# Wide attention of layer 1: value rows as the stationary side, 512 turned probabilities as the moving side

## The reference, cut to what matters

```python
q = (query @ Wq + bq).reshape(b, sq, N_HEAD, KEY_DIM)
k = (key @ Wk + bk).reshape(b, key.shape[1], N_HEAD, KEY_DIM)
v = (value @ Wv + bv).reshape(b, value.shape[1], N_HEAD, VALUE_DIM)
scores = jnp.einsum('bqhd,bkhd->bhqk', q, k) / TEMP
attn = jax.nn.softmax(scores, axis=-1)
out = jnp.einsum('bhqk,bkhd->bqhd', attn, v).reshape(b, sq, N_HEAD * VALUE_DIM)
out = out @ Wo + bo + residual
mu = jnp.mean(out, axis=-1, keepdims=True)
var = jnp.var(out, axis=-1, keepdims=True)
return (out - mu) * jax.lax.rsqrt(var + EPS) * ln_gamma + ln_beta
```

## Time and profile before

| | |
|---|---|
| median of 3 runs | 1587.16 us (1586.48 to 1588.48) |
| the profiled execution, its own time | 1588.14 us |
| its span | 1586.3 us |
| TensorE matmul busy | 1302.4 us (82%) |
| VectorE, ScalarE, GpSimd busy | 954.0 us, 716.6 us, 533.3 us |
| mean granted TensorE clock | 0.894 of full speed |
| layer 1 attention in the span | 286 us to 601.5 us |

### The profile page before, as it was taken

How to read it: one execution, slowest core, us unless ns; L and a number is a source line. 1 busy time by engine, 2 the same in 40 slices (tenths; PEclk the granted TensorE clock), 3 DMA queues, 4 the chain that set the end, 5 groups by cost and what they waited for, 6 DMA issues and landing times. The chain is left out here.

```text
span 1586.3 us, 26220 instructions
## 1 busy us (share of the span) xinstructions
PE 1302.4 (82%) x9426; PEld 800.9 (50%) x9426; DVE 954.0 (60%) x2171; ACT 716.6 (45%) x1922; POOL 533.3 (34%) x625
## 2 busy tenths in 40 slices
PE   3799629679989877786996798989987978996998
PEld 2444317457767765464442455555644434442443
DVE  6466631455656654267564688888674865655664
ACT  3254413266656523343543465656655333454222
POOL 2320250534333251334000365657543320000444
PEclk8599859799999987896998799999987996998999
DMA  2444020330000002322000000000000001000000
GB/s 63 125 135 127 30 78 26 70 81 11 1 1 2 1 24 66 88 60 50 16 3 1 1 1 1 1 1 1 1 1 1 1 11 21 10 2 1 7 7 14
DMA packets 66997, 45.37 MB, mean 29 GB/s; under 512 B 17564, under 2 KB 60262, under 8 KB 66870
## 3 DMA queue, kind: packets, MB, share of 16 engines
q1 hardware_dynamic: 61013, 34.48, 8.4%
q0 software_dynamic: 4096, 8.40, 2.1%
q10 hardware_dynamic: 1760, 0.82, 0.3%
HBM read 24.91 MB, written 13.89 MB: 24 GB/s over the span
## 5 line engine op out<-in xcount | busy, mean ns | idle before, releaser
L3413 ACT ACTIVATE L2a_pr<-psum,L2a_negmax 128x512 f32<-128x512 f32 (+3 forms) x256 | 132.2, 531 | 94.0 <-DVE L2a_negmax L3539 40.1
L556 ACT ACTIVATE L1x_praw<-psum,L1x_negmax 128x154 f32<-128x154 f32 x256 | 96.2, 390 | 78.1 <-DVE L1x_negmax L649 78.1
L318 POOL TENSOR_TENSOR L1x_pm<-L1x_praw,L1x_total 128x1024 f32<-128x1024 f32 x32 | 60.8, 1899 | 161.2 <-DVE L1x_total L655 138.2
L3278 PE MATMUL psum<-ident,L2a_pr 128*128 128x128 f32 x640 | 87.7, 282 | 20.2 <-DVE L2a_pT L3552 12.9
L3278 PEld LDWEIGHTS psum<-ident,L2a_pr 128*128 128x128 f32 x640 | 73.1, 145 | 25.9 <-issue 23.4
L1980 POOL TENSOR_TENSOR L3f_scaled<-L3f_sg,L3f_wide 128x512 f32<-128x512 f32 (+1 forms) x44 | 55.8, 1272 | 66.8 <-ACT L3f_sg L2059 37.9
L1613 DVE TENSOR_REDUCE L3x_negmax<-psum 128x6 f32<-128x924 f32 (+1 forms) x48 | 47.7, 1011 | 46.7 <-PE psum L1151 37.4
L1613 DVE TENSOR_REDUCE L0x_negmax<-psum 128x6 f32<-128x924 f32 (+1 forms) x48 | 47.7, 1009 | 44.9 <-PE psum L1151 40.6
L419 PE MATMUL psum<-L1x_vw,L1x_pT 128*128 128x128 f32 x512 | 69.8, 293 | 3.0 <-DVE L1x_y L672 3.0
L3166 POOL TENSOR_TENSOR L2a_pr<-L2a_pr,L2a_total 128x768 f32<-128x768 f32 x32 | 48.7, 1522 | 69.9 <-DVE L2a_total L3568 69.7
L3163 POOL TENSOR_TENSOR L2a_pr<-L2a_pr,L2a_total 128x1024 f32<-128x1024 f32 x29 | 56.6, 1951 | 46.1 <-DVE L2a_total L3568 46.0
(11 more groups left out here) (741 smaller groups left out, 3406.3 us busy)
## 6 DMA issues: line engine op xcount, KB each, us to landing
expert_arena<-in_L_ffn_w SPq DMA_DIRECT2D x16, 256.0 KB, 4.5
group_in<-zero SPq DMA_DIRECT2D x2, 1472.0 KB, 9.3
L1f_xs<-group_in SPq DMA_DIRECT2D x10, 256.0 KB, 4.0
group_out<-L1f_ys SPq DMA_DIRECT2D x10, 256.0 KB, 2.3
L1f_gu<-in_L_ffn_gate_up_w SPq DMA_DIRECT2D x8, 256.0 KB, 3.4
slots_in<-zero SPq DMA_DIRECT2D x1, 1280.0 KB, 9.3
L0f_xs<-slots_in SPq DMA_DIRECT2D x5, 256.0 KB, 3.9
resid<-in_x SPq DMA_DIRECT2D x4, 256.0 KB, 5.9
```

The costliest lines, as they stand in the source:

```text
L318: nc.gpsimd.tensor_tensor(pm[:, n % 2].rearrange("p j t k -> p (j t) k"), praw[:, n % 3, :, :, 0:MAIN].rearrange("p j t k -> p (j t) k"), ...
L556: nc.scalar.activation(praw[:, n % 3, j, t, :], psum[:, 2 * u + j, x * CTX:(x + 1) * CTX], ACT.Exp, bias=negmax[:, n % 2, u, j, x:x + 1], ...
L3278: last = nc.tensor.transpose(psum[:, TURN + n // 4, n % 4 * P:(n % 4 + 1) * P], pr[:, m % RING, n * P:(n + 1) * P], core.ident[:])
L3413: ins = nc.scalar.activation(pr[:, i % RING, SEQ * j + lo:SEQ * j + hi], psum[:, bank + j, lo:hi], ACT.Exp, bias=negmax[:, i % RING, e:e + ...
```

## The change

The roles of the two operands of the value products are exchanged. The table `vw` of a head (128 context rows by 128 columns) becomes the stationary side, and the turned probabilities `pT` (128 context rows by 512 query rows) move past it in one go. One product takes the place of four, and the sum in OUT is turned: columns of the output on the partitions, the 512 rows of the batch along them.

Because OUT is turned, the bias is one number a partition. ScalarE adds it in a new step `output(b)`, which copies OUT to `yT` in SBUF (a part of `core.x1` that this stage doesn't otherwise use); the bias products go. A new TensorE step `rows_back(b)` turns `yT` back with four transpositions into bank IN, and L672 reads IN in place of OUT. `values` at g = 0 waits for `yo` (ScalarE's copy) in place of `yr`, and the `query` after it waits for `yr`, as its bank is IN.

```diff
-        bo = sb("bos", [1, D])
+        bo = sb("bos", [P, 1])
...
+        yT = core.x1[:].rearrange("p n d -> p (n d)")[:, NG * KP:NG * KP + SEQ]
...
                     if g == 0 and b:
-                        pe.wait_ge(s["yr"], b)
+                        pe.wait_ge(s["yo"], b)
                     for j in range(G):
-                        for t in range(QT):
-                            last = nc.tensor.matmul(psum[:, OUT, t * P:(t + 1) * P], pT[:, m % 3, j, t * P:(t + 1) * P], vw[:, b % 2, g, j, :],
-                                                    start=(g == 0 and t == 0 and j == 0), stop=False, skip_group_check=True)
+                        last = nc.tensor.matmul(psum[:, OUT, :], vw[:, b % 2, g, j, :], pT[:, m % 3, j, :], start=(g == 0 and j == 0), stop=False)
                     if g % 2:
                         pe.wait_ge(s["tt"], m // 2 + 1)
-                        for t in range(QT):
-                            last = nc.tensor.matmul(psum[:, OUT, t * P:(t + 1) * P], tT[:, t * P:(t + 1) * P], vwt[:, b % 2, g // 2, :],
-                                                    start=False, stop=False, skip_group_check=True)
-                    if g == NG - 1:
-                        if b == 0:
-                            pe.wait_ge(s["bo"], 1)
-                        for t in range(QT):
-                            last = nc.tensor.matmul(psum[:, OUT, t * P:(t + 1) * P], core.ones[0:1, :], bo[0:1, :],
-                                                    start=False, stop=True, skip_group_check=True)
+                        last = nc.tensor.matmul(psum[:, OUT, :], vwt[:, b % 2, g // 2, :], tT[:], start=False, stop=(g == NG - 1))
                     last.then_inc(s["pv"], 1)
+                def rows_back(b):
+                    pe.wait_ge(s["yo"], b + 1)
+                    for t in range(QT):
+                        last = nc.tensor.transpose(psum[:, IN, t * P:(t + 1) * P], yT[:, t * P:(t + 1) * P], core.ident[:])
+                    last.then_inc(s["yt_ps"], 1)
...
                 for g in range(NG):
-                    last = nc.tensor.matmul(psum[0:1, OUT, 0:D], w["bv"][:, g:g + 1], w["wo"][:, g * P:(g + 1) * P], start=(g == 0), stop=(g == NG - 1))
+                    last = nc.tensor.matmul(psum[:, OUT, 0:1], w["wo"][:, g * P:(g + 1) * P], w["bv"][:, g:g + 1], start=(g == 0), stop=(g == NG - 1))
...
                         turned(m)
+                    if b and b < B and g == 3:
+                        if follows:
+                            pe.wait_ge(s["q"], n + NG)
+                        rows_back(b - 1)
                     if n < NS:
                         scores(n, 1)
                     if 0 <= n - 3 < NS:
                         values(n - 3)
                     if n < NS and follows:
                         pe.wait_ge(s["q"], n + NG)
+                        if b and g == 3:
+                            pe.wait_ge(s["yr"], b)
...
+                rows_back(B - 1)
                 grouped.experts(pe, 0)
...
+                def output(b):
+                    act.wait_ge(s["pv"], NG * (b + 1))
+                    if b == 0:
+                        act.wait_ge(s["bo"], 1)
+                    if b:
+                        act.wait_ge(s["yt_ps"], b)
+                    nc.scalar.activation(yT, psum[:, OUT, :], ACT.Identity, bias=bo[:, 0:1]).then_inc(s["yo"], 1)
...
+                    if b and g == 2:
+                        output(b - 1)
                     if b and g == 4:
                         root(b - 1)
+                output(B - 1)
                 root(B - 1)
...
-                        dve.wait_ge(s["pv"], NG * (b + 1))
-                        nc.vector.tensor_tensor(y[:], psum[:, OUT, :].rearrange("p (t d) -> p t d", d=D), xn[:, b % 3], ALU.add).then_inc(s["yr"], 1)
+                        dve.wait_ge(s["yt_ps"], b + 1)
+                        nc.vector.tensor_tensor(y[:], psum[:, IN, :].rearrange("p (t d) -> p t d", d=D), xn[:, b % 3], ALU.add).then_inc(s["yr"], 1)
...
-                nc.vector.tensor_tensor(bo[:], psum[0:1, OUT, 0:D], w["bo"][:], ALU.add).then_inc(s["bo"], 1)
+                nc.vector.tensor_tensor(bo[:], psum[:, OUT, 0:1], w["bo"][:], ALU.add).then_inc(s["bo"], 1)
...
-        load(L, w, sem, "bo", [1, D], row(io["L1_xattn_bo"]))
+        load(L, w, sem, "bo", [P, 1], io["L1_xattn_bo"].rearrange("(d o) -> d o", o=1))
```

More of the change, by code:

```diff
@@ L249, in wide_attention @@
         "bq", "pad", "vec", "xn", "xt_ps", "xt", "q_ps", "q", "k_ps", "k", "vt_ps", "vt", "vw_ps", "vw", "sc", "mx", "ex", "rs", "nm", "nt",
-        "tr", "pt", "tt_ps", "tt", "pv", "yr", "yvar", "ysd", "bo_ps", "bo", "rvar", "rsd", "summed")}
+        "tr", "pt", "tt_ps", "tt", "pv", "yo", "yt_ps", "yr", "yvar", "ysd", "bo_ps", "bo", "rvar", "rsd", "summed")}
     back = [nc.alloc_semaphore(f"{L}_back{b}") for b in range(B)]
```

## The result

The change made the kernel faster by more than I forecast: 1572.69 us median of 4 runs (1570.2 to 1574.66) against 1587.18 (1586.48 to 1588.48), a ratio of 0.9907 with a 95% interval of 0.989 to 0.9924. That is 14.5 us where the sum said 8.35; the time lies 1.3 us under the low end of the range. The two profiled executions took 1588.14 and 1570.20 us, 17.94 apart: the one of the kernel after was its fastest, the one of the kernel before was near its slowest, so the profiles show 3.4 us more than the medians.

A forecast was written before the change was run, and what follows sets the result against it. TensorE's own list was taken as nearly the bound of the stage. Value products 4.3, bias products 2.2, the L672 wait 1.75 and the start 0.1 sum to 8.35 us: 1578.8 against the median, range 1574 to 1584.

The forecast's parts named there:

- the sum: Whole kernel: 4.3 + 2.2 + 1.75 + 0.1 = 8.35 us saved, giving 1578.8 us against the median.
- Rival D: Full clock holds at 461.9 and step 28, 1.7 us each, or step 26 gives 1.3: 10 to 13 us saved; 10%.
- C: Rival on TensorE's clock: more steps fall to half clock, about 1.7 us per stretch, so the kernel gets slower; 5%.
- Value products: TensorE before 557 us: wide products save 0.17 us per even pair, 0.21 per odd, together 4.3, between 0 and 7.
- Bias products: TensorE, 1.08 us each of four; two on the path (steps 10 and 18), so 2.2 us saved.
- The wait for L672: Steps 11, 19, 27: 1.01 us TensorE idle goes, 0.43 of transpositions comes; 1.75 us saved, 0.9 to 3.0.
- Steps 15, 23 and 26: Savings lost to VectorE and ScalarE chains; TensorE idle grows from 1.55 to 1.7 us, at step 26 from 0.31 to 1.6.
- Start and end: Bias row at the start saves 0.1 us; VectorE's last part comes 0.0 to 0.3 later, against 2.9 of cover.
- A: Rival: other chains absorb more of the per-step savings, leaving 4 to 6 us saved, 1581 to 1583.5 us; 15%.
- B: Rival: no measurable change; the bias steps are absorbed too, 1.75 and 0.1 us stay, 1585.3 us; 8%.

The follow-up runs named there:

- filled pair: Kernels before and after, each with four useless identity transpositions put into TensorE's idle time in up to four steps of a batch: 1578.95 and 1572.37 us.
- filled kernel: Kernel after with four useless identity transpositions put into TensorE's idle time in up to four steps of a batch: 1572.37 us, ratio 0.9912.
- pair with the delay: Kernel after with five empty VectorE steps ahead of the stage's first sum, without and with useless transpositions in TensorE's idle time: 1579.78 and 1572.55 us.
- narrow kernel: Kernel after with each wide value product cut into four of 128 moving columns on the same stationary side: 1579.0 us, ratio 0.9964.

## Why the prediction was wrong

The sign was right, and so was what the change does to TensorE's list. Two terms failed. The profiled difference of 17.94 us is 6.4 of the change's own, 4.6 of clock between the same two maxima, 0.2 in the rest of the stage, 5.7 behind the stage and 1.0 ahead of it. With the own part alone the time would have been 1587.2 - 6.4 = 1580.8 us, within the range.

**Sum, the clock left at nothing.** This is the step that failed. The prediction made its sum against one profiled execution and carried that execution's half-clock stretches over unchanged; those that might go were a rival of 10%, priced for two places in the stage, and the 984.8 us of unchanged code behind it had no term at all. Rival D is what happened in the stage: the full clock holds at 461.9 (1.57 us, by how far the products on its two sides moved) and at step 28, where the values ran at half clock (3.0 with what stands around them), 4.6 where D had 1.7 each. The time came out below D's 1574 to 1577 as well, for want of the term behind the stage. The prediction weighed C against D by what the change does to idle stretches. The runs show something else in its place: the kernel before stood in an unfavourable place. It was 8 us slower than with a delay and 7 slower than with its idle time filled, and all five edits made to it here moved it down, by 5 to 10 us. One profile couldn't give that, but a term of several microseconds either way, for the clock of the whole program, could have stood beside the sum.

**Value products, 4.3 forecast.** Some 2.0 measured: 0.07 an even pair and 0.11 an odd one, for 0.17 and 0.21. The price was taken from rows where one wide product follows another: 1.72 without a seam was held against 1.89 with one, and 0.10 of the 0.17 was the seam, which stays.

**Bias products, 2.2.** 2.56: the seams again, here gone with the products.

**The wait for L672, 1.75.** 1.9 as the rest of the 6.4. In the filled pair VectorE's steps come 0.65, 0.69 and 0.65 us earlier at the three changes of batch, the values of that step with them: idle time of 1.01 gone, four transpositions in. Nothing idles before `rows_back`.

**Steps 15, 23 and 26.** Lost, as the prediction has it, but at another idle stretch: the time before 440.35 stayed at 1.54, and the 0.07 saved turn up ahead of it, where the tails' transpositions wait for VectorE's copy, 0.15 us in the kernel before and 0.23 after:

```profile
440.84 0.63 PE L407 MATMUL psum<-ident,L1x_pt 128*128 128x128 f32 x4 [0.15 <-DVE L1x_pT L662]
```

```profile
436.93 0.63 PE L408 MATMUL psum<-ident,L1x_pt 128*128 128x128 f32 x4 [0.23 <-DVE L1x_pT L678]
```

In step 26 the half clock at 519.07 hid the idle time; without it (filled kernel) it is 1.66, with 1.6 forecast.

**Start and end.** The bias row took 1.84 us instead of 1.91, 0.07 for 0.1. The end followed GpSimd: from the end of its last scatter to the next stage it is 4.95 us, and 4.94 in the kernel before. VectorE ended with more cover than before (5.50 us to the next stage for 4.23):

```profile
583.50 0.96 POOL L2776 DMA_INDIRECT group_in<-L1x_got,slot_of  x1 [0.31 <-issue]
```

```profile
583.74 0.17 DVE L792 TENSOR_SCALAR stat<-L1x_mv 128x8 f32<-128x8 f32 x1
589.41 0.17 DVE L2626 TENSOR_SCALAR std<-stat 128x8 f32<-128x8 f32 x1 [5.50 <-PEq L3840]
```

**Rivals.** A and B fell: no other chain absorbed more. C fell: mean clock rose. At two places (456 in the pair with the delay, 519) the clock held with four added transpositions of the identity where it fell without them. By the Trainium skill, TensorE: Matmul & The Clock Gate, Part 4: PE-mode transpose, transpositions don't count as activity for the clock in the same way; these two places speak against that. As an estimate, the same section's 275 ns as a rate would have made `rows_back` 1.1 us; it is 0.53 (402.11 to 402.64).

**What stays open.** Why the clock falls at one of many like idle stretches and not at another wasn't found, nor what moved it in the kernels with empty steps, whose entry into the stage differed by up to 2.9 us from each other's already ahead of the edit. The clock's part behind the stage was not the aim of any run: for 3.7 of the 5.7 us three rows with equal work show it, for the rest it is concluded. And the difference of the medians of the filled kernels is 6.6 us without and 3.7 with the delay: in the stage the change's own part is known to a few tenths, in the whole time to some 2 us only.

## What to carry to other kernels

Where TensorE bounds a kernel and its clock falls now and then, one profile of one version is a sample: compare an edit in two or three placements (with a small delay, with idle time filled), since the placement moved this kernel by 8 us and the edit by 4 to 7. Measure the edit between two instructions of its own stage, in profiles whose clock held there: that gave the same 6.4 us in every placement. Price a product by rows in which it has the same neighbours, seams included. Useless products in idle time that nothing waits for are a cheap way to make a time robust; here they gave the kernel after nothing measurable (1572.37 for 1572.69), but saved it 7 us in an unfavourable placement.

## What the runs showed of the hardware that was not expected

- Five empty VectorE steps, 0.8 us together, went with a change of the whole program by -8 us (before) and +6 us (after).
- Half-clock places repeated within a microsecond in two profiles of one kernel, in the changed stage.
- float32 products of 512 columns save only 4% over four of 128 with the same data (1.82 for 1.89). A change in the number of stationary rows (64 to 128, 1 to 128) costs some 0.10 us on each side; a change of the moving width alone costs nothing that shows.
- One-row bias products cost more than full ones: eight instructions take 1.08 us, and 0.20 more on the neighbours, where eight of 128 stationary rows take 0.89 (398.82 to 399.71 in the narrow kernel).
